# Tiles of a four-block transformer kernel moved from boundaries of 32 bytes to boundaries of 64

## The chip, the core and the metric

The kernel runs on one core of a Trainium2 chip. The metric is device time in microseconds (us), from one launch; lower is better. The core has TensorE (PE), VectorE (DVE), ScalarE (ACT), GpSimd (POOL) and SyncE (SP, which here only issues transfers), 128 partitions of SBUF, eight banks of PSUM, and 16 DMA engines.

## What is computed

Sixteen batches of 256 tokens with 256 features pass through four residual blocks, all in float32:

```python
x = x + L0_xattn(layernorm(x), ctx)   # argmax memory, then 16 heads of width 16
x = x + L0_ffn(layernorm(x))          # 8 experts of 1024 hidden, top 2, GELU
x = x + L1_xattn(layernorm(x), ctx)   # own layernorm, 16 heads of width 64, softmax, output matrix, gate
x = x + L1_ffn(layernorm(x))          # 32 x 4 small experts, each group of 32 tokens dealt out by a maximum
```

## The kernel before, in words

`X`, the 4096 tokens as 128 partitions x 32 x 256 floats, stays in SBUF from start to end. Each engine has its own instruction list, written out by hand in slots; engines wait for each other only through semaphores, and between the four phases all five meet (`phase_end`).

1. **L0 attention** (to about 450 us): 128 slots, eight for a batch. In each slot PE computes scores (L397), DVE takes row maxima (L557), and eleven slots later PE computes the scores turned (L409), ACT takes the exponential (L668) and PE multiplies by the values (L420). Tokens and one-hots are turned by PE (L445, L472, L499, L491) and taken out of PSUM by ACT (L689, L705, L710). POOL splits the context into a high and a low part (L744, L746) and splits weights in the same way (L750, L752).
2. **Routing, with keys and values of L1** (450 to 690 us): PE runs L348 and L354.
3. **Experts** (690 to 1140 us): 39 tiles of 256 tokens, their weights fetched by index into two buffers each, `WE1` and `WE2`, split by ACT (L1182, L1188) and DVE (L1233, L1238), multiplied by PE (L1151, L1165).
4. **L1 attention** (1150 to 1800 us) and then the **small experts** (1780 us to the end). At the end, results go to DRAM (`rp_scratch<-RP`), come back in another order (`R<-rp_scratch`, tiles `R2`), and PE returns them to their tokens (L1518, L1521); DVE adds (L1623) and ACT's queue stores the sum from `XO`.

SBUF is laid out by the class `Arena`: a running address `at`, and for each tile its bytes in a partition, rounded up. Arenas are started anew at `base1`, just behind the tiles that are kept throughout, once for each phase, and at fixed distances behind it; so tiles of different phases lie over each other.

The addresses that come out before the change (bytes within a partition): the first arena starts at 16512, which is 258 x 64. The kept tiles are multiples of 64 long until `WIX` (40 x 4 = 160 bytes, two and a half times 64), so that `base1` is 55840, which is 32 past a multiple of 64. Most tiles are whole multiples of 64 long (1, 2, 4 or 8 KB), so a whole phase keeps this remainder until a short tile changes it. Of 224 tiles, 169 start 32 bytes past a boundary of 64, and 55 start on one. On one are: `X`, `CST` (constants with the identity), the small kept tiles, in L0 everything from `OH` on (behind the 8 bytes of `MIF`): `OHT`, `MKS`, `MVV`, `PT0`, `OT`, `ON`, `ONT`, `CHL`; `WE21`, the second of the two buffers `WE2` (each 9248 bytes, 144.5 x 64); `BO`, `BOS`, `ONER`; and `X3T`, `PB3`, `LT3`. Off it are: `WQ`, `CT`, `XNa`, `XNTa`, `QT`, `QS`, `CHR`, `W1K`, `WS`, `KVS`, `XNF`, both `WE1` and the first `WE2` (`WE20`), all of `W1P`, `W2P`, `XRP`, `HP`, `YS`, and nearly everything of L1 (`GY`, `XN1`, `KS`, `XNP`, `W1Q`, `Q1`, `K1`, `W1O`, `OT1`, `V1`, `P1`, `PT1`, `PX`, `RP`, `R2`, `XO`).

Of the kernel before, what the change touches and what calls it, by code (L numbers as in the profile page):

```python
# [18 lines left out]
class Waits:  # L19


    def __init__(self, e):
        self.e, self.passed = e, {}
# [20 lines left out]

class Arena:

    def __init__(self, nc, at):
        self.nc, self.at = nc, at

    def __call__(self, name, shape, dt):  # L50
        size = int(np.prod(shape[1:])) * (2 if dt == mybir.dt.bfloat16 else 4)
        t = self.nc.alloc_sbuf_tensor_at(name, shape, dt, offset=self.at)
        self.at += (size + 31) // 32 * 32
        return t


# [2131 lines left out]
```

## Time and profile before

| | us |
|---|---|
| median of three runs | 2019.84 (2010.23 to 2020.27) |
| the profiled execution, its own time | 2005.15 |
| its span, first to last instruction | 2003.3 |

The profile is of the one execution that took 2005.15 us; 1.85 us of it lie outside the span. "Busy" is time in which an instruction ran on an engine; PEclk is the TensorE clock that was granted, as a share of full speed; the DMA share is the mean busy share of the 16 DMA engines. "Min/median/max" are durations in ns of one instruction. In a row of PE the names read out<-moving,stationary. `P<-P` and the like leave buffer numbers out.

### The profile page before, as it was taken

The page shows a single profiled execution, that of the slowest core. Times are in us where ns is not written, and L with a number is a line of the kernel's source. Part 1 is how long each engine was busy: PE and PEld are TensorE (multiplying, and loading weights), DVE is VectorE, ACT ScalarE, POOL GpSimd, SP SyncE. Part 2 cuts the span into 40 slices and gives each one's busy share as a digit, 9 for nine tenths or more (in the row PEclk, how much of TensorE's full clock was granted, in tenths as well). Part 3 has the DMA queues.
Part 4 walks back from the last instruction along what each step waited for, and adds up shares of the span by engine and source line. Part 5 has one row for each costly group of instructions (what it writes and reads, how often), then busy time and mean ns, then how long its engine had stood idle before and what let it go on. Part 6 is the DMA issues. An engine that isn't in the chain of part 4 may idle for free.

```text
span 2003.3 us, 41308 instructions
## 1 busy us (share of the span) xinstructions
PE 1785.9 (89%) x15920; PEld 1480.6 (74%) x15920; DVE 1418.4 (71%) x2887; ACT 1131.2 (56%) x2812; POOL 779.1 (39%) x1160
## 2 busy tenths in 40 slices
PE   4788888888999899999999848999999999997647
PEld 3555656656999799999999836777787787876523
DVE  3667777774231498989889668999999999766421
ACT  1254545552344487777777547777777777743310
POOL 1212221101000233333332168788888887654100
PEclk9799999999999999999999969999999999998866
DMA  6444444423658567676677332222222221112599
GB/s 191 106 79 82 86 86 86 80 70 117 218 201 314 183 232 252 230 248 247 227 250 242 105 116 91 64 82 68 64 83 67 64 82 57 52 46 86 189 365 328
DMA packets 132054, 292.27 MB, mean 146 GB/s; under 512 B 13009, under 2 KB 77138, under 8 KB 116882
## 3 DMA queue, kind: packets, MB, share of 16 engines
q1 hardware_dynamic: 109458, 179.75, 29.1%
q0 software_dynamic: 18048, 105.69, 15.3%
q10 hardware_dynamic: 4352, 4.20, 0.6%
q8 instruction: 126, 2.06, 0.4%
q14 instruction: 70, 0.57, 0.1%
HBM read 203.60 MB, written 85.72 MB: 144 GB/s over the span
## 4 chain that ended last, share of the span: by engine, by line
PE 71%; DVE 13%; DMA 5%; issue 5%; POOL 3%; ACT 2%; SPq 0%; POOLq 0%; DVEq 0%
PE ps L1151 10%; PE ps L1165 10%; PE ps L1727 5%; PE ps L348 5%; PE ps L354 4%; PE ps L213 4%; PE ps L1758 4%; PE ps L1747 4%; PE ps L1713 4%; DVE NM L557 2%; PE ps L420 2%; DVE NM L179 2%; DMA R<-rp_scratch 2%; PE ps L463 2%; PE ps L409 2%
## 5 line engine op out<-in xcount | busy, mean ns | idle before, releaser
L190 ACT ACTIVATE P<-ps,NM 128x256 f32<-128x256 f32 x512 | 235.6, 473 | 162.1 <-DVE NM L179 161.4
L203 POOL TENSOR_TENSOR P<-P,RS 128x1024 f32<-128x1024 f32 x128 | 245.2, 1916 | 93.9 <-DVE RS L197 93.5
L557 DVE TENSOR_REDUCE NM<-ps 128x2 f32<-128x512 f32 x256 | 164.7, 686 | 107.4 <-PE ps L397 107.2
L1151 PE MATMUL ps<-XRP,W1P 128*128 128x256 f32 x1872 | 226.9, 281 | 3.0 <-DVE W1P L1233 3.0
L668 ACT ACTIVATE PT<-ps 128x512 f32<-128x512 f32 x256 | 138.7, 593 | 150.2 <-PE ps L409 147.8
L1151 PEld LDWEIGHTS ps<-XRP,W1P 128*128 128x128 f32 x1872 | 220.1, 190 | 3.6 <-DVE W1P L1233 3.6
L1165 PE MATMUL ps<-W2P,HP 128*128 128x256 f32 x1872 | 221.3, 277 | 0.0
L1165 PEld LDWEIGHTS ps<-W2P,HP 128*128 128x128 f32 x1872 | 217.7, 188 | 0.0
L137 POOL TENSOR_TENSOR LTMP<-RSTD 128x2 f32<-128x2 f32 (+1 forms) x156 | 33.2, 213 | 351.4 <-DVE RSTD L130 343.1
L179 DVE TENSOR_REDUCE NM<-ps 128x2 f32<-128x512 f32 x256 | 164.2, 683 | 1.0 <-PE ps L1713 0.4
L1095 POOL DMA_INDIRECT WE<-in_we,WIX x39 | 44.2, 1134 | 300.4 <-DVE W1P L1233 198.9
L1197 ACT ACTIVATE HF<-ps,WE 128x256 f32<-128x256 f32 x312 | 129.0, 465 | 44.8 <-PE ps L1151 44.8
L1713 PEld LDWEIGHTS ps<-K,Q 64*128 64x128 f32 x1536 | 100.1, 187 | 58.3 <-issue 45.3
L220 ACT ACTIVATE PT<-ps 128x512 f32<-128x512 f32 x256 | 139.9, 610 | 1.0 <-PE ps L213 1.0
L1727 PE MATMUL ps<-PT,V 128*64 128x256 f32 x1024 | 138.8, 392 | 1.2 <-DVE OT L1844 1.2
L213 PE MATMUL ps<-CST,P 128*128 128x128 f32 x1024 | 134.6, 274 | 1.6 <-ACT PT L220 1.6
L1713 PE MATMUL ps<-K,Q 64*128 64x256 f32 x1536 | 126.6, 298 | 9.5 <-DVE Q L1836 9.0
L948 ACT ACTIVATE KVS<-ps 128x512 f32<-128x512 f32 x110 | 65.3, 597 | 109.5 <-PE ps L348 52.5
L1188 ACT ACTIVATE W2P<-WE 128x512 fp32r<-128x512 f32 x156 | 97.3, 624 | 52.0 <-PE ps L1165 52.0
L1747 PE MATMUL ps<-XNP,W1Q 128*128 128x256 f32 x768 | 112.0, 297 | 14.9 <-POOL XNP L1992 14.9
L1091 POOL DMA_INDIRECT XR<-xn_scratch,RIX x78 | 79.8, 1023 | 105.7 <-DVE RIX L1082 69.3
L213 PEld LDWEIGHTS ps<-CST,P 128*128 128x128 f32 x1024 | 113.3, 140 | 7.1 <-issue 1.9
(217 smaller groups left out, 3881.1 us busy)
## 6 DMA issues: line engine op xcount, KB each, us to landing
k_scratch<-KVS SPq DMA_DIRECT2D x64, 256.0 KB
v_scratch<-KVS SPq DMA_DIRECT2D x64, 256.0 KB
KS<-k_scratch SPq DMA_DIRECT2D x64, 256.0 KB
V<-v_scratch SPq DMA_DIRECT2D x16, 1024.0 KB
rp_scratch<-RP SPq DMA_DIRECT2D x16, 1024.0 KB
R<-rp_scratch SPq DMA_DIRECT2D x16, 1024.0 KB, 14.0
QS<-q_scratch SPq DMA_DIRECT2D x96, 128.0 KB, 4.4
ys_scratch<-YS SPq DMA_DIRECT2D x39, 256.0 KB
```

What stands on the lines that cost most here:

```text
L179: e.tensor_reduce(self.NM[:, u % 4, 2 * x:2 * x + 2], PS[SB[n % 3]][:, :].rearrange("p (h j) -> p h j", h=2), AX.X, ALU.max, negate=True). ...
L190: i = e.activation(self.P[u % 4][:, c, :], PS[SB[n % 3]][:, y * 256:y * 256 + 256], ACT.Exp, bias=self.NM[:, u % 4, c:c + 1], accum_out=se ...
L203: e.tensor_tensor(p, p, self.RS[:, u % 4, :].unsqueeze(2).to_broadcast([128, 4, 256]), ALU.mult).then_inc(self.s_pn, 1)
L213: i = e.transpose(PS[TB[h]][:, c0:c0 + 128], self.P[u % 4][:, c, jt * 128:jt * 128 + 128], ident)
L220: e.activation(self.PT[u % 4][h][:, :], PS[TB[h]][:, :], ACT.Copy).then_inc(self.s_tv, 1)
L557: e.tensor_reduce(NM0[b % 2][:, :, 8 * h + p], PS[SB[(2 * u + h) % 3]][:, :].rearrange("p (l j) -> p l j", l=2), AX.X, ALU.max, negate=Tru ...
L668: e.activation(PT0[u % 4][h][:, :], PS[TB[h]][:, :], ACT.Exp).then_inc(s_ex0, 1)
L1151: m = e.matmul(PS[p][:, hh * 256:hh * 256 + 256], W1P[i % 2][wi][:, cc * 1024 + hc * 128:cc * 1024 + hc * 128 + 128], XRP[i % 2][xi][:, cc ...
L1165: m = e.matmul(PS[4 + k][:, s * 256:s * 256 + 256], HP[k][hi][:, hc, s * 128:s * 128 + 128], W2P[k][wi][:, hc * 256:hc * 256 + 256], start ...
L1713: m = e.matmul(PS[SB[(2 * u + h) % 3]][:, lt * 256:lt * 256 + 256], Q1[i][64 * h:64 * h + 64, p, lt * 128:lt * 128 + 128], K1[j][64 * h:64 ...
L1727: m = e.matmul(PS[OB][64 * h:64 * h + 64, 0:256], V1[b % 2][:, jt, (2 * p + h) * 64:(2 * p + h) * 64 + 64], a1.PT[u % 4][h][:, jt * 256:jt ...
L1747: m = e.matmul(QB[:, j * 256:j * 256 + 256], W1Q[wi][:, cc, c0:c0 + 128], XNP[b % 2][xi][:, cc, :], start=(cc == 0 and x == 0), stop=(cc = ...
```

## The change

`Arena` rounds its start, and the size of each tile, up to 64 bytes instead of 32. No instruction, wait, queue or size of an operand is changed.

```diff
 class Arena:
 
+
     def __init__(self, nc, at):
-        self.nc, self.at = nc, at
+        self.nc, self.at = nc, (at + 63) // 64 * 64
 
     def __call__(self, name, shape, dt):
         size = int(np.prod(shape[1:])) * (2 if dt == mybir.dt.bfloat16 else 4)
         t = self.nc.alloc_sbuf_tensor_at(name, shape, dt, offset=self.at)
-        self.at += (size + 31) // 32 * 32
+        self.at += (size + 63) // 64 * 64
         return t
```

## Rows read from the trace of the kernel before

**Rows 1.** The page: span, TensorE's busy time, granted clock by fortieths.
```profile
span 2003.3 us, 41308 instructions
...
PE 1785.9 (89%) x15920; PEld 1480.6 (74%) x15920; DVE 1418.4 (71%) x2887; ACT 1131.2 (56%) x2812; POOL 779.1 (39%) x1160
...
PEclk9799999999999999999999969999999999998866
```

**Rows 2.** Busy time by stretch; last columns granted clock, DMA share, GB/s.
```profile
300.00:450.00 150.00, 133.06 (x1156) 90.12 (x1152) 106.91 (x252) 79.66 (x163) 21.20 (x80) 1.00 0.37 79
...
700.00:1100.00 400.00, 398.23 (x3473) 398.00 (x3472) 359.11 (x598) 311.83 (x669) 143.06 (x138) 1.00 0.69 241
...
1200.00:1800.00 600.00, 584.37 (x5203) 467.60 (x5201) 525.59 (x1078) 428.75 (x1372) 462.99 (x611) 1.00 0.22 69
...
1960.00:2003.00 43.00, 35.00 (x228) 14.08 (x220) 8.26 (x12) 0.00 (x0) 0.00 (x0) 0.62 0.95 323
```

**Rows 3.** The chain that ended last, pieces near the end: start, us, what.
```profile
1929.78 8.38 DMA rp_scratch<-RP
1938.32 5.93 DMA R<-rp_scratch
...
1950.22 15.09 DMA R<-rp_scratch
...
1976.00 14.34 DMA R<-rp_scratch
```

**Rows 4.** Single lines of ACT, DVE and POOL: duration ns min/median/max.
```profile
L1182 ACT ACTIVATE W1P<-WE x156: 612/620/632, 689.0 to 1123.8; 128x512 fp32r<-128x512 f32 x156
...
L1188 ACT ACTIVATE W2P<-WE x156: 613/622/637, 691.7 to 1133.7; 128x512 fp32r<-128x512 f32 x156
...
L705 ACT ACTIVATE OHT<-ps x16: 597/597/597, 32.0 to 420.8; 128x512 f32<-128x512 f32 x16
...
L689 ACT ACTIVATE XNTa<-ps x16: 597/597/605, 19.3 to 406.9; 128x512 f32<-128x512 f32 x16
...
L598 DVE TENSOR_SCALAR MKS<-ps,CST x16: 534/536/544, 36.3 to 426.6; 128x256 fp32r<-128x256 f32 x16
...
L1830 DVE TENSOR_SCALAR XNP<-ps,GB x32: 528/534/536, 1167.5 to 1721.8; 128x256 fp32r<-128x256 f32 x32
...
L592 DVE TENSOR_SCALAR OH<-CST,MIF x32: 345/350/355, 30.2 to 419.7; 128x256 f32<-128x256 f32 x32
...
L149 DVE TENSOR_SCALAR XNF<-X,MV,RSTD x32: 395/402/412, 501.4 to 511.4; 128x256 f32<-128x256 f32 x32
...
L746 POOL TENSOR_TENSOR CHL<-CT,CHL x16: 1261/1269/1272, 16.7 to 385.4; 128x512 fp32r<-128x512 f32 x16
...
L752 POOL TENSOR_TENSOR W1K<-WS,W1K x8: 1262/1272/1282, 54.8 to 232.8; 128x512 fp32r<-128x512 f32 x8
```

**Rows 5.** TensorE in order of time, at full granted clock: start, us, instruction.
```profile
297.08 0.50 PE L397 MATMUL ps<-MKS,QS 48*128 48x256 f32 x4
...
299.43 0.50 PE L409 MATMUL ps<-QS,MKS 49*128 49x256 f32 x4
...
1304.81 0.50 PE L1762 MATMUL ps<-BOS,ONER 1*128 1x256 f32 x2
```

**Rows 6.** Two lines of TensorE that turn a tile: duration ns min/median/max.
```profile
L213 PE MATMUL ps<-CST,P x1024: 270/273/331, 1194.4 to 1781.9; 128*128 128x128 f32 x171
...
L491 PE MATMUL ps<-CST,OT x128: 270/273/333, 104.4 to 487.4; 128*128 128x128 f32 x128
```

**Rows 7.** Stretches with many transfers, columns as in rows 2.
```profile
7.00:10.00 3.00, 0.00 (x0) 0.00 (x0) 1.36 (x5) 0.00 (x0) 0.00 (x0) 1.00 0.99 360
...
74.00:80.00 6.00, 5.12 (x48) 3.52 (x48) 5.25 (x13) 3.19 (x7) 0.00 (x0) 1.00 1.01 324
...
1904.00:1930.00 26.00, 12.20 (x128) 8.21 (x128) 10.31 (x16) 8.69 (x16) 0.00 (x0) 0.80 1.01 423
...
1965.00:2000.00 35.00, 30.96 (x200) 12.67 (x200) 6.68 (x11) 0.00 (x0) 0.00 (x0) 0.62 0.99 336
```

## The prediction

> **What bounds the kernel now.** The page comes first: TensorE is busy 89% of a span of 2003.3 us, at a granted clock of nine tenths or more nearly everywhere but the start, the change of phase near 1150 us and the end [rows 1]. The stretches come next, because a share over the whole span hides them. In the expert phase TensorE is busy 398.23 of 400 us, and the DMA engines 0.69 of it, so a transfer or a DVE instruction a few per cent longer or shorter changes nothing there. In L1 attention TensorE is busy 584 of 600 us, with DVE at 526 close behind and DMA at 0.22. L0 attention has TensorE at 133 of 150 us [rows 2]. Last comes the chain near the end, since there the picture is another one: from about 1903 us on the long pieces are transfers, first `rp_scratch<-RP` and then `R<-rp_scratch`, single waits of 6 to 15 us [rows 3], while the DMA engines are 0.95 busy and TensorE runs at 0.62 of its clock [rows 2].
>
> So an address could matter in three places only: where TensorE reads operands (about 1,100 us of phases in which it has hardly a gap), where DVE or POOL stand in TensorE's way in the two attentions, and in the last 100 us, where the DMA engines set the pace.
>
> **What the change does.** It removes and adds no instruction, wait or transfer. It moves tiles: `WIX` takes 192 bytes instead of 160, so `base1` goes from 55840 to 55872, and all 169 tiles that stood 32 bytes past a boundary of 64 now stand on one; the other 55 move by 0, 64 or 128 bytes and stay on one. No tile shrinks, and no phase meets another in a new place: the distances between arenas are whole kilobytes and short tiles add at most 128 bytes in all (`attn_at`, under the buffers of the last phases, goes from 159840 to 159936). The whole sum therefore is: instructions of each kind, times what a start at 64 instead of 32 saves each. That saving never has to be guessed, because the kernel before already holds both kinds of tiles doing the same operation.
>
> - **ACT, output.** The same copy of 128x512 out of PSUM takes 597 ns (median) into `OHT`, on a boundary, and 597 ns into `XNTa`, off one [rows 4]. Saving: 0.
> - **ACT, input from SBUF.** L1182 reads only tiles off the boundary (both `WE1`): 612/620/632 ns. L1188 reads `WE20` off and `WE21` on a boundary, half of its 156 each: 613/622/637 [rows 4]. If starting on the boundary saved time, the second row would have a lower minimum or a wider spread; it has neither. Saving: 0, at most 2 ns.
> - **DVE, output.** Two-scalar operations from PSUM, 256 wide: 536 ns into `MKS` (on), 534 ns into `XNP` (off) [rows 4]. Saving: 0.
> - **DVE, input.** There is no clean pair with both ends in SBUF. The nearest: L592, constants to `OH`, both on a boundary, 350 ns; L149, `X` (on) to `XNF` (off), 402 ns [rows 4]. The difference of 52 ns is the outer bound for a saving; I take 0, because the two rows differ also in their scalars (L592 has one, L149 two), and because an output off the boundary cost nothing in the row above.
> - **POOL.** The difference of 512 elements takes 1269 ns for `CHL` (output and second input on, first input off) and 1272 ns for `W1K` (all off) [rows 4]. Two of three operands changed and 3 ns came of it: 3 ns x 232 instructions of the kinds that read whole tiles (128 of L203, 64 of L1987, 32 of L1992, 8 of L752) is 0.7 us of POOL's time in all, most of it beside TensorE's 584 of 600 us. Saving: 0 to 0.7 us.
> - **TensorE.** Turning 128x128 takes 273 ns from `P` (off) and 273 ns from `OT` (on) [rows 6]. Of the fast float32 products, two rounds of 256 columns take 0.50 us with `MKS` moving (on) and `QS` standing (off), 0.50 us the other way round, and 0.50 us with `BOS` and `ONER`, both on a boundary [rows 5]. Saving: 0. The bound: in the expert phase 3473 products share 398.23 us [rows 2], 114.7 ns each, and 256 columns at 2.4 GHz are 106.7 ns. If all that lies above the columns were the address, 8 ns x 3473 = 28 us could go. Rows 5 speak against it, though their third group has one row of operands only.
> - **DMA.** The rate of one engine is GB/s divided by the share and by 16. With pieces of 1 KB out of DRAM that land in `X`, on a boundary, mixed with splits going out, it is 324 / 1.01 / 16 = 20.0; with 1 KB pieces into `R2` and out of `XO`, both off, 336 / 0.99 / 16 = 21.2; at the start, with 1 and 2 KB pieces, mostly into tiles off the boundary, 360 / 0.99 / 16 = 22.7; and with 8 KB pieces out of `RP`, off, 26.2 [rows 7]. The rates go with the length of the piece; the stretches off the boundary are not the slow ones. Saving: 0.
>
> A rule that would make addresses matter at all is easy to look for. The Trainium skill, in "SBUF — State Buffer", section "Operand start alignment", asks only for a start at a multiple of the element's size, and says that this is "about legality, not speed". All tiles before satisfy it, and no row here shows a price beside it; the sum would be 0 by it as well.
>
> The sum is thus 0 us (POOL's 0.7 us at most left aside): the profiled execution would again take 2005.15 us, 2003.3 of it span. The runs shown are 2010.23, 2019.84 and 2020.27, so executions of one program lie up to 0.75% above the profiled one. The median of 2019.84 sits at the upper end of these four values, so I forecast 2018 us for the median after: no change, and a little of that asymmetry.
>
> **Rivals.**
>
> *Longer transfers at the end (slower).* 64 is not the widest boundary there is. `R2` and `XO` stood at 96 bytes past a multiple of 256 (159840 and 208992), and stand at 192 past one afterwards; `RP2` to `RP5` likewise. If a transfer is charged for the bytes between the 256 boundary below and its start, each piece carries 96 more. From rows 7, an engine moves 32 bytes in 32 / 26.2 = 1.22 ns and a piece of 1 KB takes 1024 / 21.2 = 48.3 ns; 3 x 1.22 = 3.7 ns on it is 7.6%. The stretch that `R` bounds, 1938 us to the end, is 62 us: 4.7 us. The 8 KB pieces of `RP` get 3 parts in 256, 1.2% of 46 us: 0.6 us. Together 5.3 us, 2010.5 us for the profiled execution, 0.26%. Elsewhere it hides under TensorE. It decides the sign as soon as the charge exists, and passes 0.5% only if it were twice as large. Against it: at the start, pieces go mostly to tiles 32 past a 256 boundary, in `X` to 128 past one, and no order of rates by this distance shows [rows 7]. Chance 5%. This is the rule of the Trainium skill in "DMA: Bandwidth & Descriptors", section "How a descriptor splits into AXI transactions": a transaction must start on a multiple of 256 bytes, and the bytes before the start are fetched for nothing. By it the change would be slower; the trace, as far as rows 7 tell, does not bear it out.
>
> *DVE gains where both ends are in SBUF (faster).* Were the 52 ns an effect of the address, the 128 normalisations of L149 would save 6.7 us. All on the path, that is 1998.5 us for the profiled execution, -0.33%. For it: DVE is busy 526 of 600 us in L1 [rows 2]. Against it: the output test above, and the different scalars. Chance 5%.
>
> *TensorE gains in fast float32 products with both operands on a boundary (faster).* The 28 us above for the expert phase: 1977 us, -1.4%, and more in the other phases. Against it: rows 5 and 6. Chance 3%.
>
> *The change does not do what it says.* It does for every tile's start; operands inside tiles start at multiples of 1 or 2 KB, or at small columns, as before. What can fail is only that the start has no price, which is the forecast.
>
> **How the numbers follow.** A measurement of this kernel tells about 0.5% (10 us) from no change. The forecast holds 87%. Within it the scatter of the medians alone (the runs before span 10 us) carries a result past 0.5% now and then, rather to the low side because the median before sits high: 7% faster, 4% slower. With 3% from TensorE's case, half of a per cent from DVE's and as much from the transfers' rival: faster 0.10, same 0.85, slower 0.05. The range takes the profiled execution's own time at its low end, 2004 us, and adds the 5.3 us of the slower rival and some scatter to 2020.27 at the high end: 2029 us.
>
> **What would show it.** In the profile after, every median in rows 4 and 6 should stand within 3 ns, the groups of rows 5 at 0.50 us, and 700 to 1100 us again at some 3470 products. Transfers: 1965 to 2000 us again at about 336 GB/s per full share; a rate of 312 would be the slower rival, L149 on `XNF` at 350 ns the faster one. If the time differs by more than 0.5% with all these rows unchanged, the difference lies in gaps or in the granted clock, and my step that durations are all that an address can touch has failed.

## The result, and the profile after

The kernel became slower: 2025.94 us median of 17 runs (2021.61 to 2034.89) against 2015.22 us of before in 17 runs (2002.84 to 2020.27), ratio 1.006 with a 95% interval of 1.0043 to 1.0078. The forecast was 2018 us and no change, its range 2004 to 2029 us. The time itself lies in that range, but the change of 10.7 us between the medians is clear of the scatter and just beyond the 0.5% that the forecast took for the limit of no change, on the side that had been given one chance in twenty.

The profiled execution took 2029.15 us. Line numbers after are one higher than before, and in some of the experiments a few higher; the text names lines as the kernel before has them. The page of the changed kernel answers to [rows 1]:

```profile
span 2027.3 us, 41308 instructions
...
PE 1807.9 (89%) x15920; PEld 1500.9 (74%) x15920; DVE 1418.7 (70%) x2887; ACT 1132.0 (56%) x2812; POOL 789.5 (39%) x1160
...
PEclk9799999999999999999999969999999999998767
```

DVE and ACT worked as long as before, within 0.9 us, and POOL 10.4 us longer (experiment 7 shows that this is not what costs time). TensorE was busy 22 us longer with the same 15920 products, at nearly the same granted clock (0.950 of full speed against 0.955 over the span). The busy time by stretch of the changed kernel says where; its first line answers to the second of [rows 2], the second is the whole expert phase, from the first product of L1152 to the last of L1166:

```profile
700.00:1100.00 400.00, 397.88 (x3350) 397.64 (x3350) 345.24 (x574) 301.27 (x646) 148.81 (x137) 0.99 0.67 232
...
697.40:1163.20 465.80, 463.67 (x3892) 463.26 (x3892) 394.93 (x656) 342.37 (x735) 158.05 (x144) 0.99 0.64 220
```

3350 products fit into the 400 us in which there had been 3473; the prediction had named some 3470 as the sign that it held. The same phase of the kernel before:

```profile
693.70:1144.70 451.00, 449.19 (x3892) 448.75 (x3892) 395.04 (x656) 342.56 (x735) 149.19 (x144) 1.00 0.65 227
```

So 14.8 us of the 24 us between the two profiled executions lie in this phase, with equal work of DVE (395 us) and ACT (342 us) and no gap on TensorE (463.67 busy of 465.80). It is the single product that grew. In this phase products come in series of 48 of one line: L1151 multiplies the tokens by the first weights, L1165 by the second. TensorE in order of time shows them, first of the kernel before, then of the changed one (start, us, instruction):

```profile
921.31 5.90 PE L1151 MATMUL ps<-XRP,W1P 128*128 128x256 f32 x48
927.05 5.82 PE L1165 MATMUL ps<-W2P,HP 128*128 128x256 f32 x48
...
933.06 5.70 PE L1151 MATMUL ps<-XRP,W1P 128*128 128x256 f32 x48
938.60 5.61 PE L1165 MATMUL ps<-W2P,HP 128*128 128x256 f32 x48
...
944.40 5.70 PE L1151 MATMUL ps<-XRP,W1P 128*128 128x256 f32 x48
949.94 5.61 PE L1165 MATMUL ps<-W2P,HP 128*128 128x256 f32 x48
```

```profile
945.41 5.93 PE L1152 MATMUL ps<-XRP,W1P 128*128 128x256 f32 x48
951.18 5.85 PE L1166 MATMUL ps<-W2P,HP 128*128 128x256 f32 x48
...
957.23 5.94 PE L1152 MATMUL ps<-XRP,W1P 128*128 128x256 f32 x48
963.00 5.85 PE L1166 MATMUL ps<-W2P,HP 128*128 128x256 f32 x48
```

Between the ends of two products of a series the records give about 113.5 ns (5.61 and 5.70 us) or 117.8 ns (5.82 and 5.90) before, the slower pace in one expert tile out of three, and 118.6 ns (5.85 and 5.93) in nearly every one after. At 2.4 GHz 256 columns are 106.7 ns, so what lies above them went from 7 or 11 ns to 12.

One more line lost a little: of 62 series of L1758 in L1 attention, 29 ran at 114 to 115 ns before and none below 118 after, which is about 1.5 us if half of its 768 products took 4 ns more (an estimate). The stretch from the first to the last scores of L1 took 594.4 us after, against 591.6 before. The other parts differ by what they also differ by between executions of layouts that do not touch them: the last products of L420 in L0 attention ended at 482.2 us before and 485.8 after, and anywhere from 480.7 to 490.6 in the traces below.

### The profile page after: what moved, and what is told of

Same layout as the page of the kernel before. It is cut to its first block, busy times and chain, and to the rows that moved or that the text cites. A ratio compares the mean times of both kernels' runs of the same rounds, so it can differ in the third digit from the quotient of the medians.

```text
span 2027.3 us, 41308 instructions
## 1 busy us (share of the span) xinstructions
PE 1807.9 (89%) x15920; PEld 1500.9 (74%) x15920; DVE 1418.7 (70%) x2887; ACT 1132.0 (56%) x2812; POOL 789.5 (39%) x1160
## 4 chain that ended last, share of the span: by engine, by line
PE 70%; DVE 13%; DMA 6%; issue 5%; POOL 3%; ACT 2%; SPq 0%; POOLq 0%; DVEq 0%; ACTq 0%
PE ps L1152 10%; PE ps L1166 10%; PE ps L1728 5%; PE ps L349 4%; PE ps L214 4%; PE ps L1759 4%; PE ps L355 4%; PE ps L1748 4%; PE ps L1714 4%; PE ps L421 2%; DMA R<-rp_scratch 2%; DVE NM L558 2%; DVE NM L180 2%; PE ps L464 2%; PE ps L410 2%
## 5 line engine op out<-in xcount | busy, mean ns | idle before, releaser
L1152 PE MATMUL ps<-XRP,W1P 128*128 128x256 f32 x1872 | 234.5, 285 | 3.4 <-DVE W1P L1234 3.4
L1152 PEld LDWEIGHTS ps<-XRP,W1P 128*128 128x128 f32 x1872 | 227.3, 191 | 4.0 <-DVE W1P L1234 4.0
L1166 PE MATMUL ps<-W2P,HP 128*128 128x256 f32 x1872 | 228.1, 281 | 0.0
L1166 PEld LDWEIGHTS ps<-W2P,HP 128*128 128x128 f32 x1872 | 224.7, 188 | 0.0
L1092 POOL DMA_INDIRECT XR<-xn_scratch,RIX x78 | 88.6, 1136 | 106.4 <-DVE RIX L1083 69.7
```

The costliest lines, as they stand in the source:

```text
L1152: m = e.matmul(PS[p][:, hh * 256:hh * 256 + 256], W1P[i % 2][wi][:, cc * 1024 + hc * 128:cc * 1024 + hc * 128 + 128], XRP[i % 2][xi][:, cc ...
L1166: m = e.matmul(PS[4 + k][:, s * 256:s * 256 + 256], HP[k][hi][:, hc, s * 128:s * 128 + 128], W2P[k][wi][:, hc * 256:hc * 256 + 256], start ...
```

## What could be the cause

**Theory A.** What counts is the distance of a product's two operands, stationary minus moving start, modulo 256. The offsets of the kernel before and after, worked out from `Arena`:

| product | stationary - moving | before | after |
|---|---|---|---|
| L1151, experts up | `W1P` - `XRP` | 64 | 128 |
| L1165, experts down | `HP` - `W2P` | 192 | 128 |
| L348, L1747, L1713 | `W1K` - `CHR`, `W1Q` - `XNP`, `Q1` - `K1` | 0 | 0 |
| L1758 | `OT1` - `W1O`, one batch and the next | 64 and 0 | 128 and 0 |

The short tiles that are rounded up lie between the two operands (two `WE2` in the first two rows, `GB` and `TG` in the last), so their padding changed the distance. **Theory B.** A start on a boundary of 64 costs TensorE time by itself. **Theory C.** The difference is scatter. **Theory D.** Other engines, reading and writing SBUF meanwhile, collide with TensorE in the new place.

## Experiments

The kernel before ran again beside the experiments, so the time that stands against an experiment's is of those runs. A ratio is worked out from all times and can differ from that of the two medians by 0.001 or 0.002. Two experiments with TensorE alone, and two repeats of a profile, have one execution each.

**1. All tiles but the kept ones moved by 32.** No distance between the moved tiles changes; `X`, `CST` and the small tiles kept throughout stay. To the kernel before:

```diff
+    keep.at += 32
     base1 = keep.at
```

> The kernel before with one line added: base1 is moved by 32 bytes, so that every tile but the ones kept throughout moves by the same 32 bytes. All of XRP, HP, W1P, W2P, W1Q, XNP, W1O, Q1, K1 now start on a boundary of 64, as in the changed kernel, but the distance between any two of them is that of the kernel before. Theory A (what counts is the distance of the two operands of one product, taken modulo a small power of two; in the expert phase it was 64 modulo 256 and became 128): nothing changes. Experts from the first product of L1151 to the last of L1165 451 us as before, not 466; ratio 1.000 within 0.003. Theory B (a start on a boundary of 64 by itself is what costs TensorE time): experts near 466 us, ratio 1.006. Theory C (the difference is scatter and place in the time of the run): 451 us, and the ratio as A.

Measured: 2006.33 us against 2012.82 us, ratio 0.9963 (0.9935 to 0.9990). Busy time in the expert phase:

```profile
696.10:1144.10 448.00, 446.07 (x3892) 445.63 (x3892) 395.28 (x656) 342.67 (x735) 144.51 (x144) 0.99 0.66 229
```

Both operands of L1151 and of L1165 now stand on boundaries of 64, and the phase takes 448.0 us, not 466. B is out. It is even 3 us faster than before, since the slow series in every third tile are gone; A had not foreseen that, nor that the ratio would come out below 0.997.

**2. The weights alone moved by 64.** Before, with:

```diff
     mem_i = Arena(nc, mem.at)
+    mem.at += 64
     W1P = [[mem(f"W1P{i}{j}", [128, 2048], f32r) for j in range(2)] for i in range(2)]
```

> The kernel before, with only W1P and W2P (the split expert weights) moved by 64 bytes. All tiles keep their 32 bytes past a boundary of 64; the distance of weights and tokens in the products of the expert phase becomes 128 modulo 256, as in the changed kernel. Theory A: the expert phase takes 466 us instead of 451, some 118.6 ns for a product instead of 113 to 118, ratio 1.006 to 1.008. Theory B: no tile is on another boundary of 64, so 451 us and ratio 1.000. Theory C: ratio 1.000.

Measured: 2022.09 us against 2012.82 us, ratio 1.0039 (1.0017 to 1.0061). The expert phase:

```profile
693.00:1157.60 464.60, 463.50 (x3892) 463.05 (x3892) 395.05 (x656) 342.36 (x735) 158.13 (x144) 0.99 0.64 220
```

Most of the loss (13.6 of 14.8 us in this phase), and on TensorE the same pace of 118.6 ns, with every tile's remainder at 64 as it was. The distance was 64 and 192 and is 128, as in the changed kernel. C is out. The ratio stayed under the 1.006 expected.

**3. TensorE alone, 19 pairs of offsets.** Only the core of the kernel is shown:

```python
m = e.matmul(PS[k % 8][:, i % 2 * 256:i % 2 * 256 + 256], ST[so][:, c * 128:c * 128 + 128],
             MT[mo][:, i % 2 * 256:i % 2 * 256 + 256], start=True, stop=True)   # c = i % 8
```

> Not the reference's computation: TensorE alone does 96 fast float32 products of 128x128 by 128x256 for each of 19 pairs of start offsets (moving, stationary; bytes past a multiple of 8192), three visits to each; all else is left out. Theory A: the time of a product goes by the difference of the two offsets: near 120 ns at difference 0, 113 to 118 at 64, 118 to 119 at 128, the same for (0, 64), (32, 96) and (64, 128). Theory B: it goes by each offset's remainder at 64: (32, 32) is faster than (0, 0) and (64, 64). Theory D (other engines that read and write SBUF meanwhile are what the address brings TensorE into conflict with): all pairs take the same time, since nothing else works here.

TensorE in order of time; MAA, MBB, MCC move at 0, 32, 64, and SAA, SBB, SCC, SDD, SEE, SFF, SGG stand at 0, 32, 64, 96, 128, 160, 192:

```profile
88.56 11.68 PE L57 MATMUL ps<-MAA,SEE 128*128 128x256 f32 x96
...
168.85 11.67 PE L57 MATMUL ps<-MBB,SBB 128*128 128x256 f32 x96
180.36 11.52 PE L57 MATMUL ps<-MBB,SCC 128*128 128x256 f32 x96
191.72 11.47 PE L57 MATMUL ps<-MBB,SDD 128*128 128x256 f32 x96
203.03 11.55 PE L57 MATMUL ps<-MBB,SFF 128*128 128x256 f32 x96
214.41 11.47 PE L57 MATMUL ps<-MCC,SAA 128*128 128x256 f32 x96
225.72 11.68 PE L57 MATMUL ps<-MCC,SCC 128*128 128x256 f32 x96
237.24 11.06 PE L57 MATMUL ps<-MCC,SEE 128*128 128x256 f32 x96
```

From the start of a series to the start of the next, a product takes 120 ns at distance 0 (MBB with SBB, MCC with SCC), 118 at 32, 118 at 64 with moving offset 32 and 113.6 with 64, 118.5 at 128. Distances of 256, 512 and 1024 gave 120 ns as 0 did, which is why the distance is taken modulo 256. No other engine works, so the difference needs none and D is out; offsets alike in their remainder at 64 differ, so B again. The records of single products at distance 128 even repeat the changed kernel's own sequence (116, 116, 122 or 123, 118, 121 ns). But 64 came out at two values, which the theory as stated doesn't explain, and (0, 128) gave 120 where (32, 160) gave 118.5. All three visits, in one order, gave each pair the same pace.

**4. A map, in three orders.** The same with 48 products for each of 32 pairs, visited in three different orders, and then four series of 48 with 32 stationary columns.

> Not the reference's computation: TensorE alone, 48 products of 128x128 by 128x256 for each of 32 pairs of offsets (four moving, and for each eight distances of the stationary operand from 0 to 224 bytes), in three different orders, and then 48 products with only 32 stationary columns at distances 0, 64, 0, 64. Theory A: distance 0 gives 120 ns a product whatever the two offsets and whatever came before; distance 64 and 192 give 113 to 118; distance 128 gives 118 to 120; if the same pair comes out at two different times in the three orders, then the state in which a series starts counts as well, which would explain why one expert tile in three took 118 ns before and the others 113. If it is the reading of the stationary columns that collides with the moving ones, then 32 columns in place of 128 leave at most a third of what lies above the 106.7 ns of 256 columns, and distance no longer matters much.

Time of one product in ns, mean of the last 36 of each series, over four moving offsets (0, 32, 64, 96) and three visits:

| stationary - moving, modulo 256 | ns of a product |
|---|---|
| 0 | 119.9 to 120.0 |
| 32 | 118.1 to 118.5 |
| 64 | 113.3 to 113.6 in ten of twelve, 117.7 and 117.8 in two |
| 96 | 117.3 to 118.8, once 120.1 |
| 128 | 118.6 to 118.9 |
| 160 | 119.8 to 120.1 |
| 192 | 117.7 or 117.8 in ten, 113.3 and 113.4 in two |
| 224 | 116.5 to 117.8 |

The same pair in two visits, at 192 (MCC moves at 64, SAA stands at 0), and one row each of distance 0 and 64:

```profile
114.24 5.92 PE L59 MATMUL ps<-MAA,SAA 128*128 128x256 f32 x48
...
210.60 5.60 PE L59 MATMUL ps<-MCC,SAA 128*128 128x256 f32 x48
...
272.62 5.81 PE L59 MATMUL ps<-MCC,SAA 128*128 128x256 f32 x48
...
357.43 5.62 PE L59 MATMUL ps<-MCC,SEE 128*128 128x256 f32 x48
```

and the series with 32 stationary columns, at distances 0 and 64:

```profile
583.93 5.62 PE L72 MATMUL ps<-MAA,SAA 128*32 128x256 f32 x48
589.39 5.60 PE L72 MATMUL ps<-MAA,SCC 128*32 128x256 f32 x48
```

The distance sets which paces occur, whatever the two offsets. At 64 and 192 a series can run at either of two, and after its first products keeps its pace to the end; 96 and 224 have more than one as well, and 128 has, with the 120 ns of experiment 3. That the same pair differs between orders, while experiment 3 in one order repeated every pace, suggests that what came before decides; experiment 5 will show that it is not that alone. With 32 stationary columns distances 0 and 64 no longer differ: 113.3 ns each. This fits a collision of the load of the next weights with the moving columns, but does not show it: such a product also has only 32 rows of output, and no width between 32 and 128 was tried. The expectation that only a third would be left above 106.7 ns was too low, 6.6 ns are. The expectation for 64 and 192 held.

**5. The changed kernel with its distance put back.** The change itself, all tiles on boundaries of 64, and:

```diff
     mem_i = Arena(nc, mem.at)
+    mem.at += 192
```

> The changed kernel (all tiles on boundaries of 64) with W1P and W2P moved on by 192 bytes, so that the distance to the tokens in the products of the expert phase is 64 modulo 256 again; everything stays on a boundary of 64. Theory A: the expert phase goes back from 466 us to 448 to 451 us, and the whole time to within 0.4% of the kernel before: 2010 to 2020 us. Theory B (a start on 64 costs TensorE time) and any theory that blames the rest of the change: 466 us and the time of the changed kernel, near 2026 us.

Measured: 2011.73 us against 2011.80 us, ratio 1.0006 (0.9978 to 1.0034): the loss is gone in the median. But the profiled execution had 463.0 us of experts, where 448 to 451 were expected, and the ten times fell into two groups, seven from 2006.99 to 2013.68 us and three from 2022.70 to 2030.83. So the same program was run again for a second profile:

> The third experiment once more, for a second profile of the same program. Its ten times fell into two groups, seven from 2007 to 2014 us and three from 2023 to 2031, and the profiled one was in the second, at 117.8 ns a product. Theory A with two states: this time, with 7 chances in 10, experts at 448 to 451 us with L1151 and L1165 at 113 ns and a time below 2015 us; else again 463 us. If the two groups have another cause, the experts take 463 us again whatever the whole time is.

The expert phase of the first execution, then of the second, which took 2007.65 us:

```profile
697.00:1160.00 463.00, 460.91 (x3892) 460.47 (x3892) 394.94 (x657) 342.21 (x735) 155.97 (x144) 0.99 0.64 221
```

```profile
692.90:1140.90 448.00, 446.03 (x3892) 445.64 (x3892) 395.42 (x656) 342.76 (x735) 145.19 (x144) 0.99 0.65 229
```

Two paces of one program, 15 us apart: in the first nearly every series of L1151 and L1165 ran at 118 ns, in the second at 113 to 114. These are the two paces of the map, each held over nearly all of the 39 expert tiles. The order of the instructions is the same in both, so it alone does not decide.

**6. The kernel before, once more.**

> The kernel before once more, unchanged, for a second profile. In its first, one series of 48 products in three took 118 ns a product and the others 113, and the experts 451.0 us. Theory A with two states: 448 to 463 us, with a share of 118 ns series of its own, and a whole time that follows it. If the pattern is fixed by the program, 451.0 us again.

2011.00 us; the experts took 452.9 us, and again every third tile ran at 118 ns, with small differences at the start and the end of the phase. Most of the 1.9 us come from the second series of L1151, which ran at 150 ns a product instead of 114. The pattern of three is largely the program's, its edges are not. What makes it three wasn't settled; `XR` has three buffers, and L1138 turns them between the series. In experiment 1, where the pattern is gone, `CST` stayed at its place, so the distance of `XR` to it in L1138 went from 160 to 192; whether that did it was not tested.

**7. Distance 0.** As experiment 2, with 192 in place of 64:

```diff
     mem_i = Arena(nc, mem.at)
+    mem.at += 192
```

> The kernel before with W1P and W2P moved on by 192 bytes, so that weights and tokens of the expert phase stand at distance 0 modulo 256 (all at 32). Theory A with the map of the run on 32 pairs (120 ns a product at distance 0, against 113 to 118 at 64): the expert phase takes 3744 x 1.2 to 6.6 ns more than the 451 us of before, 470 to 472 us, the longest of all; ratio 1.008 to 1.011. Theory B (boundaries of 64): 451 us, ratio 1.000, since no tile changes its remainder modulo 64.

Measured: 2030.92 us against 2012.96 us, ratio 1.0090 (1.0058 to 1.0123), experts 470.9 us:

```profile
702.90:1173.80 470.90, 469.07 (x3892) 468.68 (x3892) 396.58 (x656) 342.51 (x735) 144.47 (x144) 0.99 0.63 218
```

This is the slowest layout tried, as the map said, with time and ratio as expected, and no boundary of 64 plays a part in it. POOL was busy for 144 us here, less than the 149 us of before, so its longer time in the changed kernel is not the cause.

**8. 64 in both products of the experts.**

```diff
+    mem.at += 128
     W2P = [[mem(f"W2P{i}{j}", [128, 2048], f32r) for j in range(2)] for i in range(2)]
```

> The kernel before with only W2P moved on by 128 bytes. Stationary minus moving offset is then 64 modulo 256 in both products of the expert phase; before it was 64 in the first (L1151) and 192 in the second (L1165), where W2P moves. Theory A with the map (64 came out at 113.4 ns in 11 of 12 series, 192 at 117.8 in 10 of 12): nearly all series at 113.4 ns, expert phase 446 to 449 us, ratio 0.995 to 0.999 and less scatter from one execution to the next. If the sign of the distance plays no part in the kernel, 451 us and 1.000.

Measured: 2015.46 us against 2012.96 us, ratio 1.000 (0.9978 to 1.0022), experts 455.5 us. The expectation of 446 to 449 us fell. TensorE in order of time:

```profile
941.67 5.70 PE L1152 MATMUL ps<-XRP,W1P 128*128 128x256 f32 x48
947.21 5.82 PE L1166 MATMUL ps<-W2P,HP 128*128 128x256 f32 x48
```

L1151 runs at 113 ns and L1165, at the same distance of 64, at 118. The map gives the two paces that a distance allows, not which of them a series falls into behind another one.

**9. 64 in the other phases too.** Experiment 1 with, besides (lines from several places, the comments added here):

```diff
+    mem.at += 128      # before W2P
+    mem_k = Arena(nc, mem_w.at + 192)      # CHR
+    mem.at += 64       # before W1Q
+    mem.at += 192      # before K1
+    mem.at += 64       # before OT1[1]
+    mem.at += 192      # before V1 and OT1[0]
```

> The kernel of the first experiment (base1 moved by 32) with gaps of 64 to 192 bytes laid between tiles, so that stationary minus moving offset is 64 modulo 256 in all fast float32 products of the big phases: L1151, L1165, and now also keys of L348 (the values of L354 get 192), queries L1747, scores L1713 and the output matrix L1758. They stood at 0 there, but for half of L1758. Theory A: the products of L348 and L1747 fall from 120 to 114 to 118 ns, 768 each, and half of L1758's 768: the phase of keys and values 2 to 5 us shorter than 238.6 us, L1 attention 2 to 8 us shorter than 593 us, the experts 446 to 449 us. Whole time 2000 to 2008 us, ratio 0.993 to 0.997 to the kernel before. Theory B: ratio 1.006, since everything is on a boundary of 64 or moved by multiples of it.

Measured: 2005.20 us against 2012.96 us, ratio 0.9962 (0.9944 to 0.9981). Time and ratio came as expected, and so did keys and values with 236.2 us and the stretch from the first to the last scores of L1 with 588.3 us; the experts took 455.4 us as in the last experiment, not the 446 to 449 expected. Nearly all series of L1747 ran at 113 to 115 ns (119 to 120 before) and of L1758 at 113 to 114 (half of them before, the other half near 119), those of L348 partly at 114 and partly at 118 (119 to 120 before). L354, 512 columns at a time, went the wrong way: a median of 230 ns where it had been 227. So a distance of 192 isn't good for products of that form.

**10. Both together: `W2P` back at its place.**

> The kernel with 64 everywhere, with W2P back where it was, so that the distance in L1165 is 192 again. In the kernel with W2P moved, L1151 ran at 113 ns and L1165 at 118; in the first experiment, at distances 64 and 192 all on boundaries of 64, both ran at 113 and the experts took 448.0 us. Theory A with a state that one series of products hands to the next: experts 448 us instead of 455.4, the rest as in the kernel with 64 everywhere (236 us for keys and values, 588 us for L1 attention); 1996 to 2001 us, ratio 0.991 to 0.995. If the state of L1165 is decided by chance in each execution: experts at 448 or 455, and no gain on the other kernel in the median.

Measured: 2000.88 us (1993.33 to 2004.63) against 2011.12 us, ratio 0.9931 (0.9906 to 0.9956). Busy time for keys and values, the experts, and the scores of L1:

```profile
453.20:689.40 236.20, 228.15 (x1603) 201.53 (x1601) 73.98 (x179) 89.03 (x159) 19.50 (x58) 0.99 0.59 210
697.30:1145.30 448.00, 445.89 (x3892) 445.46 (x3892) 395.44 (x656) 342.78 (x735) 145.16 (x144) 0.99 0.65 229
1178.90:1767.30 588.40, 567.34 (x5069) 454.67 (x5070) 521.72 (x1064) 429.30 (x1389) 464.50 (x610) 0.99 0.21 68
```

In the kernel before these were 238.6, 451.0 and 591.6 us. All of it came as expected. This version beats both kernels, with nothing but empty bytes between tiles: 10 us faster than the one before and, by the two ratios, 1.3% faster than the changed one.

## Why the prediction was wrong

- **ACT, DVE and POOL: right in the main.** After the change three of the rows that answer to [rows 4] are

```profile
L1183 ACT ACTIVATE W1P<-WE x156: 612/619/630, 692.7 to 1141.8; 128x512 fp32r<-128x512 f32 x156
...
L150 DVE TENSOR_SCALAR XNF<-X,MV,RSTD x32: 401/405/413, 505.0 to 515.1; 128x256 f32<-128x256 f32 x32
...
L747 POOL TENSOR_TENSOR CHL<-CT,CHL x16: 1262/1271/1278, 15.8 to 387.6; 128x512 fp32r<-128x512 f32 x16
```

  620, 402 and 1269 ns before. The DVE rival needed 350 ns in the second of them. It is out: the 52 ns were not the address of the output. Three of the other rows moved by more than the 3 ns that had been allowed: the median went from 597 to 592 ns for `XNTa`, from 622 to 618 for `W2P` and from 1272 to 1279 for `W1K`. All of it is under 1 us (156 x 4 ns for `W2P`), so the term of 0 stands.
- **DMA: right.** While `R` comes back, 1990 to 2024 us, the changed kernel moved 334 GB/s at a share of 0.99; it had been 336 at 0.99 [rows 7], and the slower rival needed about 312. (The stretch that this rival was worked out on, 1938 to 2003 us, is 65 us long and not 62, which makes its 4.7 us 5.0.) The charge for bytes below a boundary of 256, as the Trainium skill gives it in "DMA: Bandwidth & Descriptors", section "How a descriptor splits into AXI transactions", does not appear here, though these tiles went from 96 to 192 past such a boundary.

```profile
1990.00:2024.00 34.00, 29.49 (x200) 11.90 (x199) 6.19 (x10) 0.00 (x0) 0.00 (x0) 0.65 0.99 334
```

- **TensorE: this step failed.** "Saving: 0", with a bound of 28 us on one side only, was the term of the sum that was wrong: it was a loss of 14.8 us in the expert phase of the profile. In its place the runs showed 4 to 5 ns a product, set by the distance of its two operands. Three things went into the error. The groups compared [rows 5] are two rounds long, so 4 ns a round are under 0.01 us, in a row that gives hundredths; and their products use 1, 48 or 49 rows of the array, a form other than that of the 3744 that matter. The products that turn a tile [rows 6] had their operands at two distances (224 for `P`, 64 for `OT`) and the same time, 273 ns, and 272 and 273 after: a control of another form. And the question was whether a tile starts on a boundary, never how two tiles of one product stand to each other. The 8 ns that were found above 106.7 were used as a bound for a gain; the same rows bound no loss, and the sum had to keep that end open. The trace of before did hold the evidence: the same line L1151 at 5.70 and at 5.90 us for 48 products, the longer in every third tile, on an engine that is busy 398 of 400 us.
- **The step "no phase meets another in a new place" was beside the point:** the prediction counted up to 128 bytes that short tiles add, and did not follow them to the pair `W1P` and `XRP`, between which 64 of them lie.
- **Centre and scatter.** The kernel before turned out at 2015.22 us, below the 2019.84 us of the first three runs, as the forecast had leaned to. That 2025.94 us still lies in the range is luck: its upper part had been made for scatter and for slower transfers, and neither is what happened. Two paces at distances 64 and 192 can make times differ, by 15 us in one program (experiment 5); how much of the scatter of the kernel before they make was not measured, its two profiles have 451.0 and 452.9 us of experts. The changed kernel scattered by 13 us, though its two large products stand at 128; the two paces seen there, 118.7 and 120 ns, would give 5 us over 3744 products (an estimate), so other causes remain.

What stays open: what decides which pace a series falls into, why every third tile was slow before, and why the distance matters at all. L0 and the last stretch were not tried one by one.

## What to carry to other kernels

On an engine that has no gaps, compare the pace of one product in long series (start to start over 48 of them) before calling an address free, and look at the two operands of a product together: here 128 x 128 by 128 x 256 fast float32 products took 113 to 120 ns by the distance of their tiles modulo 256, worst at 0. Rounding tiles up to a larger power of two is no gain in itself: by arithmetic, rounding to 256 would put every pair of tiles at distance 0, while gaps of 64 to 192 bytes, chosen by measurement, gave 0.7%. The best distance depends on the form of the product, as L354 shows. When one program's times fall into two groups, take a second profile before believing the first.

## What was not expected of the hardware

- A product with weights of its own is not free of where its two operands stand to each other: 120.0 ns at distance 0, 113.3 at best, with TensorE alone at work, and 113.3 at distances 0 and 64 with 32 stationary columns. The Trainium skill, in "SBUF — State Buffer", section "Who interferes with whom", gives TensorE two independent read ports, one for the moving operand and one for loading the weights, and says that TensorE never waits on anyone. Other engines do not come into it here, as the page has it; but by these runs the pace does depend on the two operands' addresses together.
- The pace holds on: at distances 64 and 192 a series keeps 113.3 or 117.8 ns to its end, and a whole phase can hold one of them (448.0 and 463.0 us of the same program).
- The float32 products that turn a tile (L213 before, 128x128) didn't mind the move: 273 ns for one before, 272 after, though `P` moved by 96 bytes against the identity in `CST`.
